# Batched cross-attention on one core: key rows padded to 384 and sent ahead of the query, moved rows through DRAM, opening rewritten

## The reference

```python
q, k_t, v_t = heads(x @ W_q), heads(text @ W_k), heads(text @ W_v)      # text: 371 rows
probs_t  = softmax(q @ k_t.T / 4)
text_out = probs_t @ v_t
k_ip, v_ip = heads(ip @ W_k_ip), heads(ip @ W_v_ip)
qsem  = l2norm(probs_t @ text)                                          # per head and row
fused = q @ k_ip.T / 4 + 0.5 * qsem @ l2norm(ip).T
out   = (text_out + mask * softmax(fused) @ v_ip) @ W_out + b_out + x
```

## Time and profile before

| | |
|---|---|
| median of three executions | 801.38 us |
| the profiled execution, its time and its span | 807.7 us, 805.9 us |
| mean granted TensorE clock | 0.962 |
| PE, DVE, ACT, POOL busy | 90%, 80%, 69%, 52% of the span |
| first scores of batch 0 start | 49.9 us |
| DMA engines busy, q1 (SPq) | 50.9% |

### The profile page before, as it was taken

How to read it: one execution, slowest core, us unless ns; L and a number is a source line. 1 busy time by engine, 2 the same in 40 slices (tenths; PEclk the granted TensorE clock), 3 DMA queues, 4 the chain that set the end, 5 groups by cost and what they waited for, 6 DMA issues and landing times.

```text
span 805.9 us, 22617 instructions
## 1 busy us (share of the span) xinstructions
PE 728.1 (90%) x7218; PEld 564.6 (70%) x7218; DVE 644.0 (80%) x1862; ACT 553.2 (69%) x1590; POOL 418.3 (52%) x511
## 2 busy tenths in 40 slices
PE   5449789999989999999989999999999999899882
PEld 4327567777767777777777777777777777677661
DVE  4318669798978989898978979898988989688982
ACT  4217658677766868777776868777777868567770
POOL 7003544646645565555655565555655555454651
PEclk9869989999998999999999999999999999999995
DMA  9561936546392755637393755638392744529000
GB/s 270 87 110 26 111 70 87 91 78 68 101 85 74 93 91 80 65 103 78 92 100 75 93 90 77 73 97 78 78 113 76 98 89 75 54 60 87 11 3 15
DMA packets 131492, 66.48 MB, mean 82 GB/s; under 512 B 71616, under 2 KB 131312, under 8 KB 131376
## 3 DMA queue, kind: packets, MB, share of 16 engines
q1 hardware_dynamic: 127328, 60.91, 50.9%
q10 hardware_dynamic: 4048, 4.13, 2.0%
HBM read 49.97 MB, written 14.34 MB: 80 GB/s over the span
## 4 chain that ended last, share of the span: by engine, by line
PE 55%; DMA 27%; SPq 10%; issue 3%; DVE 2%; ACT 2%; ACTq 0%; POOL 0%; DVEq 0%; POOLq 0%
PE ps_prep L564 15%; DMA k_st<-k_bounce 12%; DMA w_raw<-k_bounce 11%; PE ps_gram L662 10%; PE ps_pT L645 8%; PE ps_gram L663 7%; SPq L291 5%; PE ps_score L637 4%; PE ps_prep L619 3%; SPq L289 2%; PE ps_val L671 2%; DMA k_bounce<-k_hi 2%; PE ps_val L672 1%; PE ps_prep L594 1%; PE ps_prep L596 1%
## 5 line engine op out<-in xcount | busy, mean ns | idle before, releaser
L496 POOL TENSOR_TENSOR dual<-prob 128x371 f32<-128x371 f32 (+1 forms) x288 | 255.7, 888 | 355.0 <-ACT prob L840 350.0
L662 PE MATMUL ps_gram<-gram_hi,pT_hi 125*128 125x371 f16 (+1 forms) x864 | 274.2, 322 | 0.1
L834 ACT ACTIVATE pT_hi<-ps_pT 125x384 f16<-125x384 f32 (+1 forms) x288 | 138.8, 482 | 159.5 <-PE ps_pT L645 155.2
L663 PE MATMUL ps_gram<-gram_lo,pT_hi 125*128 125x371 f16 (+2 forms) x864 | 231.7, 269 | 0.3 <-issue 0.3
L998 DVE TENSOR_REDUCE low<-ps_score 128x1 f32<-128x371 f32 (+1 forms) x288 | 154.9, 538 | 60.4 <-PE ps_score L637 57.3
L824 ACT ACTIVATE prob<-ps_score,low 128x371 f32<-128x371 f32 (+1 forms) x288 | 165.4, 574 | 28.9 <-DVE low L998 26.3
L1003 DVE TENSOR_TENSOR pT_lo<-ps_pT,pT_hi 125x384 f16<-125x384 f32 (+1 forms) x288 | 155.0, 538 | 35.8 <-ACT pT_hi L834 31.9
L1016 DVE CUSTOM_DVE_ANT_0 quad_junk<-ps_gram,dual 128x371 f32<-128x371 f32 (+1 forms) x288 | 152.7, 530 | 5.3 <-PE ps_gram L663 2.3
L671 PE MATMUL ps_val<-val,pT_hi 125*128 125x84 f16 (+3 forms) x864 | 153.0, 197 | 0.0
L840 ACT ACTIVATE prob<-prob 128x371 f16<-128x371 f32 (+1 forms) x288 | 151.7, 527 | 0.0
L645 PE MATMUL ps_pT<-ident,prob 128*125 128x128 f32 (+1 forms) x864 | 145.1, 277 | 7.0 <-ACT prob L824 2.5
(11 more groups left out here) (181 smaller groups left out, 1491.5 us busy)
## 6 DMA issues: line engine op xcount, KB each, us to landing
ctx_sb<-in_ctx_t SPq DMA_DIRECT2D x15, 750.0 KB, 4.7
w_raw<-k_bounce SPq DMA_DIRECT2D x32, 210.9 KB, 7.8
k_st<-k_bounce SPq DMA_DIRECT2D x30, 210.9 KB, 7.5
w_raw<-k_bounce SPq DMA_DIRECT2D x64, 82.0 KB, 8.6
k_st<-k_bounce SPq DMA_DIRECT2D x60, 82.0 KB, 8.9
k_bounce<-k_hi SPq DMA_DIRECT2D x16, 281.2 KB, 3.1
k_bounce<-k_lo SPq DMA_DIRECT2D x16, 281.2 KB, 3.8
q_st<-q_bounce SPq DMA_DIRECT2D x64, 63.0 KB, 2.4
```

What stands on the lines that cost most here:

```text
L496: nc.gpsimd.tensor_tensor(dual[0:r, t % 2, :], prob[0:r, g % 4, 0:TX], prob_16[0:r, t % 2, :], ALU.subtract).then_inc(s_dual, 1)
L662: nc.tensor.matmul(ps_gram[t % 2][:, 0:TX], hi, gh[0:TROWS[i], i, :], start=(i == 0), stop=False, skip_group_check=True)
L663: last = nc.tensor.matmul(ps_gram[t % 2][:, i * TC:TX], hi, gl[0:TROWS[i], i, i * TC:TX], start=False, stop=(i == NT - 1), skip_group_chec ...
```

## The change

Four parts. (1) Key rows have a pitch of 384 elements (768 bytes) in SBUF and DRAM instead of 375 (750 bytes); the DMAs carry all 384. (2) In a batch the key pieces come first: they are made in steps 0 to 4 and taken until step 5, q is made in step 5 and taken at step 6. SP sends the keys out at step 6 and issues all twelve key DMAs at step 7, then q out at step 8 and its twelve at step 9. (3) `move_rows` becomes two DMAs to DRAM (step 14) and two back (step 15). (4) The opening makes two Gram pieces, then keys, then q; SP issues all four key terms and ACT those of q; POOL makes the lo halves of W_q and W_v and of x; the 20 small DMAs are spread over steps 1 to 11; W_v_ip, bias and mask are loaded behind the key stack.

```diff
-PIECE_Q, PIECES_K, PIECES_V, PIECES_G = 0, (1, 2, 3), (5, 7, 8), (4, 6, 9)
+PIECES_K, PIECE_Q, PIECES_V, PIECES_G = (0, 1, 2), 3, (5, 7, 8), (4, 6, 9)
-START_ORDER = (*PIECES_G, PIECE_Q, *PIECES_K, *PIECES_V)
+START_ORDER = (*PIECES_G[:2], PIECES_K[2], *PIECES_K[:2], PIECE_Q, PIECES_G[2], *PIECES_V)
-Q_OUT_STEP, Q_IN_STEP, K_OUT_STEP, K_IN_STEP, MOVE_STEP, LOAD_X_STEP = 2, 4, 7, 9, 14, 13
+K_OUT_STEP, K_IN_STEP, Q_OUT_STEP, Q_IN_STEP, LOAD_X_STEP, MOVE_OUT_STEP, MOVE_IN_STEP = 6, 7, 8, 9, 12, 14, 15
+VIP_AT = {1: 4, 2: 4, 3: 4, 4: 3, 5: 3, 10: 1, 11: 1}
+K_PITCH = T_PAD
...
-        k_hi = sb("k_hi", [P, CC, T], F16)
+        k_hi = sb("k_hi", [P, CC, K_PITCH], F16)
...
-                for j in range(XP):
-                    q0 = j * XR
-                    sp.dma_start(raw[q0:q0 + XR, NB:H, 0:2 * VW], raw[S:P, j:NBX:XP, 2 * VW:BW]).then_inc(s_moved, 16)
-                    sp.dma_start(meta[b.odd][q0:q0 + XR, NB:H, :], meta[b.odd][S:P, j:NBX:XP, :]).then_inc(s_moved, 16)
+                sp.dma_start(raw_bounce.rearrange("e j p w -> p (e j) w"), raw[S:P, 0:NBX, 2 * VW:BW]).then_inc(s_move_out, 16)
+                sp.dma_start(meta_bounce.rearrange("e j p w -> p (e j) w"), meta[b.odd][S:P, 0:NBX, :]).then_inc(s_move_out, 16)
...
+            def split_weight(n, lo, raw, hi):
+
+                pool.wait_ge(s_wsplit_hi, n + 1)
+                nc.gpsimd.tensor_scalar(raw, raw, W_UP, None, ALU.mult).then_inc(s_wscaled, 1)
+                pool.wait_ge(s_wscaled, n)
+                nc.gpsimd.tensor_tensor(lo, raw, hi, ALU.subtract).then_inc(s_wsplit_pool, 1)
...
+            split_weight(1, wq_lo[:, :, :], wq_sb[:, :, :], wq_hi[:, :, :])
+            pool.wait_ge(s_prep, 1)
+            split_lo(Batch(0, 0, 0), PIECE_X)
+            split_weight(2, w_lo[:, :, 1, :], w_raw[:, :, 1, :], w_hi[:, :, 1, :])
...
-                if k == PIECE_Q:
+                if k in (*PIECES_K, PIECE_Q) and half0 == 0:
                     pe.wait_ge(s_split_pool, len(POOL_PIECES) * (a.n + 1))
-                if k == PIECES_K[0]:
                     pe.wait_ge(s_split_lo, len(DVE_PIECES) * (a.n + 1))
```

More of the change, by code:

```diff
@@ L81, with last_key_piece, part @@
 K_IP_STEP, RESIDUAL_STEP = 1, 11
-Q_OUT_STEP, Q_IN_STEP, K_OUT_STEP, K_IN_STEP, MOVE_STEP, LOAD_X_STEP = 2, 4, 7, 9, 14, 13
+K_OUT_STEP, K_IN_STEP, Q_OUT_STEP, Q_IN_STEP, LOAD_X_STEP, MOVE_OUT_STEP, MOVE_IN_STEP = 6, 7, 8, 9, 12, 14, 15
+VIP_AT = {1: 4, 2: 4, 3: 4, 4: 3, 5: 3, 10: 1, 11: 1}
 S_PAD = P
 T_PAD = NT * P
+K_PITCH = T_PAD
+def last_key_piece(a):
+    return max(place(a, k) for k in PIECES_K)
+def part(a, k):
+    order = START_ORDER if a.n == 0 else range(NM)
+    return NL * a.n + [p for p in order if p in PIECES_G or p == PIECES_K[-1]].index(k) + 1
 def rows(t):
@@ L381, in _ @@
             load_context_weight(sp, 1)
+            sp.dma_start(ip_rows[:, :], ip[:, :]).then_inc(s_ip, 16)
             load_xt(Batch(1, 1, 0))
             load_ctx(Batch(1, 1, 0))
+            bounce_k(Batch(0, 0, 0))
+            for term in (0, 2, 1, 3):
+                bring_k(Batch(0, 0, 0), term)
             load_context_weight(sp, 3)
@@ L386, in _ @@
             sp.dma_start(mask_sb[:, :], mask.rearrange("(s a) -> s a", a=1)).then_inc(s_small, 16)
[L387 to L392, removed]
             load_rows(sp, wo_sb, w_out, s_wo)
@@ L401, in body @@
                     if b.n == 0 and t == 0:
-                        spread_v_ip()
+                        bring_v_ip()
+                    if b.n == 0 and t in VIP_AT:
+                        done = sum(VIP_AT[at] for at in VIP_AT if at < t)
+                        spread_v_ip(done, done + VIP_AT[t])
+                    if prepare and t == K_OUT_STEP:
+                        bounce_k(b.next())
+                    if prepare and t == K_IN_STEP:
+                        for term in (0, 2, 1, 3):
+                            bring_k(b.next(), term)
                     if prepare and t == Q_OUT_STEP:
                         bounce_q(b.next())
[L405 to L411, removed]
+                    if prepare and t == Q_IN_STEP:
+                        for term in range(4):
+                            bring_q(b.next(), term)
                     if prepare and t == LOAD_X_STEP:
                         load_x(b.next())
-                    if t == MOVE_STEP:
+                    if t == MOVE_OUT_STEP:
+                        rows_to_dram(b)
+                    if t == MOVE_IN_STEP:
                         move_rows(b)
@@ L443, in _ @@
                                     base=0, pattern=[[-1, P]], channel_multiplier=1).then_inc(s_const, 1)
-            for q_ in q_st:
-                nc.gpsimd.memset(q_[:, :, :], 0.0)
+            nc.gpsimd.memset(q_st[0][:, :, :], 0.0)
             nc.gpsimd.memset(k_st[0][:, NBX:NB, :], 0.0).then_inc(s_stack, 1)
@@ L453, in _, with split_lo @@
                 nc.gpsimd.memset(v[:, :, :, VW + DH:VW + DH + 1], 0.0)
+            def split_weight(n, lo, raw, hi):
[3 more added lines that the diff above has]
+                nc.gpsimd.tensor_tensor(lo, raw, hi, ALU.subtract).then_inc(s_wsplit_pool, 1)
+            def split_lo(a, k):
+                pool.wait_ge(s_split_hi, NX * a.n + k + 1)
+                if k in PIECES_TEXT:
+                    hi, lo = (t[a.odd][:, k, 0:T] for t in (text_hi, text_lo))
+                    last = nc.gpsimd.tensor_tensor(lo, ctx_sb[:, k, :], hi, ALU.subtract)
+                else:
+                    last = nc.gpsimd.tensor_tensor(x_lo[:, :, :], xt_sb[a.odd][:, :, :], x_hi[:, :, :], ALU.subtract)
+                last.then_inc(s_split_pool, 1)
+            split_weight(1, wq_lo[:, :, :], wq_sb[:, :, :], wq_hi[:, :, :])
+            pool.wait_ge(s_prep, 1)
+            split_lo(Batch(0, 0, 0), PIECE_X)
+            split_weight(2, w_lo[:, :, 1, :], w_raw[:, :, 1, :], w_hi[:, :, 1, :])
+            nc.gpsimd.memset(q_st[1][:, :, :], 0.0)
             nc.gpsimd.memset(vip_diag[:, :, :], 0.0).then_inc(s_pool_set, 1)
@@ L477, in clear_rows @@
                 pool.wait_ge(s_wsplit_hi, 3)
-                pool.wait_ge(s_wsplit_lo, 3)
+                pool.wait_ge(s_wsplit_lo, 1)
+                pool.wait_ge(s_wsplit_pool, 2)
+                pool.wait_ge(s_wk_last, 2)
                 pool.wait_ge(s_setup_pe, 3)
                 nc.gpsimd.memset(k_st[1][:, NBX:NB, :], 0.0).then_inc(s_stack, 1)
[L482 to L487, removed]
-                else:
-                    last = nc.gpsimd.tensor_tensor(x_lo[:, :, :], xt_sb[a.odd][:, :, :], x_hi[:, :, :], ALU.subtract)
-                last.then_inc(s_split_pool, 1)
             def duals(b, t):
@@ L1101, in _ @@
             start = Batch(0, 0, 0)
-            for k in range(NX):
+            for k in PIECES_TEXT:
                 split_lo(start, k)
@@ L1124, in _ @@
             last.then_inc(s_setup_ev, 1)
-            make_lo(start, PIECES_K[2], SETUP_BANKS)
-            split_weight(2, w_lo[:, :, 1, :], w_raw[:, :, 1, :], w_hi[:, :, 1, :])
+            dve.wait_ge(s_setup_ev, 2)
+            for k_, ip_ in ((k_hi, kip_hi), (k_lo, kip_lo)):
+                last = nc.vector.tensor_copy(k_[:, :, TX:T], ip_[:, :, :, 0])
+            last.then_inc(s_kip, 1)
+            for k in (PIECES_K[1], PIECE_Q, PIECES_G[2]):
+                make_lo(start, k, SETUP_BANKS)
             dve.wait_ge(s_ip, 32)
```

94 lines of the change are left out of this document (52 added, 42 removed).

## The result

The changed kernel takes **884.42 us** (median of four executions, 877.28 to 889.00) where the kernel before takes 801.17 us in the same comparison: 1.104 times as long (95% interval 1.096 to 1.113), or 83 us more. The forecast was 914 us, the range 805 to 950.

What follows compares the result with a forecast made beforehand. PE, busy 90% of 805.9 us, bounds the kernel beside its waits for the key stack. 113 (q waits and clock) + 0.7 + 1 - 2.3 = +112.4 us on 801.4 gave 914 us, range 805 to 950.

Steps and rivals of the forecast that it cites:

- the mechanism: Steady batches: q's way out lands only behind the key stack, so PE waits for q instead of keys; chance 0.80.
- what bounds the stack: Key stack's DMAs: writing 16 partitions each, not row alignment, holds them at 107 GB/s, 14.7 us with padding.
- padded rows are fast: Rival on the key stack: alignment held it down, padded it takes 6.6 us, total 764 us; chance 0.13.
- The wait: Before each steady batch's first scores: PE waits 8.1 us for q where it waited 1.3 us for keys.
- The alignment rule: Key stack: unaligned 750-byte rows cost 126 bytes more; stack 12.6 us, wait 6.0 us, total some 30 us less.
- The clock's price: After each long wait PE's clock falls to 0.50, costing 1.3 us; bounds 0 and twice that.
- Batch 1: First scores of the second batch: the wait goes from 7.4 to 8.1 us, +0.7 us.
- The opening: Program start with keys before q and the stack on one queue: +1 us, bounds -5 and +5.
- the first key piece: Opening: waits on PE for the x split on POOL behind W_q, so PE starts keys at 18 to 20 us.
- The end: Last wait for moved rows at the program's end: two short trips end sooner, -2.3 us, at worst 0.
- the case in between: Rival: alignment gives a part, stack 8 to 12.5 us, wait 1.4 to 5.9 us, 805 to 862 us; chance 0.07.

Runs made afterwards that it cites:

- Experiment 1: Changed kernel with the order in a batch undone: q made and sent first, keys after; 777.93 us, ratio 0.973 to the kernel before.
- experiment 2: Changed kernel, keys still first, but q's way out issued ahead of the twelve key DMAs back; 805.16 us, ratio 1.006 to the kernel before.
- experiment 5: DMAs only, no attention: stack-shaped loads into different partition groups, on one queue or two, rows of 768 or 750 bytes; 83 to 287 GB/s, one execution.
- experiment 6: DMAs only, no attention: one queue into 16 partitions, six combinations of row length and pitch; 77 to 101 GB/s, one execution.
- experiment 3: Changed kernel with the key rows back at their old pitch of 375, without padding; 929.13 us, ratio 1.162 to the kernel before.
- experiment 4: Changed kernel with the pitch of 384 kept, but only 375 elements (750 bytes) of each row read back into the stack; 923.94 us, one execution.
- experiment 8: Kernel before with only the key rows padded to 384; 771.16 us, ratio 0.959 to the kernel before.
- experiment 9: Kernel before with padded key rows and the moved rows through DRAM; 769.68 us, on another chip 765.66 us, ratio 0.955 on both.

## Why the prediction came out as it did

**Right: the mechanism.** PE waits for q 15 times, q's way out lands when the key stack has passed (10.1 us after issue, forecast about 12), and keys themselves are no longer waited for. Experiments 1 and 2 show it: with q's way out ahead of the stack 79 us come back, with q first 106. The time is 30 us under the forecast. By the spans the change costs 77 us where 112 were forecast: the steady periods took 40 us less and batch 1 3 us less, the opening 5 and the end 2 us more. So nearly all of the miss is the wait for q, and it looks smaller than it was, since 7 us of other misses point the other way.

**Right: what bounds the stack is mostly where it goes.** Padding lifts 107 to 121 GB/s, not to the 228 or 240 of the earlier trace rows, and experiment 5 shows the partitions at work. The rival "padded rows are fast" was 120 us off. Two things in the argument were wrong. The stack's 107 is not the rate of 16 partitions: its four terms and their small DMAs go to eight groups of 16, and one group alone takes 92 to 97 GB/s with rows of 768 bytes and 77 to 85 with 750 (experiments 5 and 6). And that the ports give one rate "whatever the rows" was my reading; those same rows show it false.

**The wait was mis-sized: 8.1 us forecast, 4.6 measured** (70.7 less batch 1's 5.9, over 14). In the batch shown: from the keys' way out to the first key DMA 3.7 forecast, 2.35 measured; from there to the landing of q's way out 17.3 forecast, 15.9 measured; q's round back 8.8 forecast, 9.1 measured. The first two are the padding, which I took at nothing: without it (experiment 3) they are 3.0 and 17.9, 21 us in all as forecast. I kept 107 GB/s because it was the row of the same DMAs and the way out ran at 240 with the same rows. The 240 showed that 750 bytes are not slow where all partitions are written from or to; it did not show that the length costs nothing where few partitions are written. Experiment 3, the same order without padding, gives 929 us: the forecast of 914 was almost one for that kernel.

The alignment rule of the Trainium skill, page "DMA: Bandwidth & Descriptors", section "How a descriptor splits into AXI transactions", would have put the total some 30 us lower, at 884. The time agrees, and so does the gain of the stack (2.1 us by that estimate, 2.0 measured); the reason does not: with all starts aligned and 750 bytes the rows stay slow (experiment 4, 924 us; experiment 6, 77 GB/s), and unaligned rows of a multiple of 4 bytes are fast (101 GB/s). The measurement decides for the length.

**The clock's price was too small: 1.3 us forecast, about 1.9 measured.** The 14 periods grew by 72.6 us, their waits by 64.8 - 18.5 = 46.3; the other 26.3 us are 1.9 each. PE's busy time shows that this is clock: windows over the 14 periods of the kernel before, that of experiment 8, the changed one and that of experiment 3.

```profile
102.81:742.35 639.54, 619.01 (x6275) 485.30 (x6275) 550.44 (x1606) 475.38 (x1380) 354.19 (x417) 0.99 0.57 84
94.15:704.93 610.78, 609.90 (x6274) 482.74 (x6275) 551.15 (x1605) 477.50 (x1380) 352.87 (x415) 1.00 0.55 89
107.31:819.46 712.15, 643.92 (x6275) 501.25 (x6275) 537.36 (x1606) 473.12 (x1380) 354.10 (x417) 0.94 0.47 77
111.96:865.34 753.38, 644.88 (x6274) 501.84 (x6275) 537.01 (x1606) 473.14 (x1380) 353.88 (x417) 0.91 0.49 72
```

The same matmuls take PE 24.9 us more than before. The kernel before had 9.1 us of slow clock itself (experiment 8), so against experiment 8's kernel the price is (643.9 - 609.9) / 14, about 2.4 us for each wait. The steps right after the waits take 3.9 to 4.9 us instead of 2.5. Forecast 14 x (8.1 - 1.3 + 1.3) = 113; measured 14 x (4.6 - 1.3 + 1.9) = 73.

**Batch 1: +0.7 forecast, -1.9 measured**; 1.5 of it is the shorter wait (5.91 against 7.36).

**The opening: +1 forecast, +6.4 measured**, outside my bound of 5. The step that failed is the first key piece at 18 to 20 us: it came at 21.85. ACT makes W_q's hi part last, so POOL starts at 15.4 instead of 13, and the scaling takes 3.13 us where I bounded it by 2.8; the subtraction took 2.36 (forecast 2.8). A scaling with one input is slower here than a subtraction with two. So the keys leave at 31.96, 3.1 us later than before (28.91). The other 3.3 us lie behind that: first scores wait for q on ACT's queue beside the stack, until 56.1, and from the keys' way out to the scores pass 24.3 us, where 20.7 were forecast and 21.0 measured before. Against the padded old order the new opening is 11 us late (56.3 against 45.0). Experiment 1 and experiment 9, which differ mainly in the opening, are 8 us apart on the same chip (777.9 and 769.7).

**The end: -2.3 forecast, -2.3 measured** for PE's last wait (10.3 to 8.0); batch 15's slow step takes most of it back.

**One bound of the prediction was mis-added.** By its own terms the case in between starts at 14 x (1.4 - 1.3) + (1.4 - 7.4) + 1 - 2.3 = -6 us, that is at 795 us and not at 805. The result is far from either.

## What to carry to other kernels

Behind a big transfer into few partitions what followed on the same queue waited here, x as well as q, and a small round trip most of all, since its second half couldn't even be issued: send the way out ahead, or the short one first. A price of nothing for an edit needs a row under the same limit; a row of other partitions did not bound what row length costs here. Try the parts of a change apart: one of them gained 4%, another cost 14%.

## What the runs showed of the hardware

- Rows of 750 bytes into 16 partitions moved at 77 to 85 GB/s, of 736 at 90 and 101, of 752 at 93 and of 768 at 92 to 97; unaligned pitches were no slower. Each is from one execution.
- In the changed kernel every wait of 3.16 us or more was followed by matmuls of 0.47 to 0.50 us and a granted clock of 0.50; shorter waits can cost it too, only later. In the kernel before, after waits of 2.12 and 2.68 us, the first matmul still took 0.33 us, but the clock fell to 0.50 some 1.2 us behind it, and the next scores came after 3.7 us instead of 2.5. The price came once for each wait and was the same for waits of 4.7 and 7.5 us on average (PE busy 643.9 and 644.9 us).
- POOL took 3.13 us to scale 1152 float32 columns in place and 2.36 us to subtract two tiles of as many; DVE made the same lo half in one instruction of 1.36 us in the kernel before.
